# Z, B and C products of a token tower: the fifth pass split into two 64-row passes per bank, two sequences' passes side by side

## The chip, the cores and the metric

The kernel runs on one core of a Trainium2 chip. The metric is the device time of one execution in microseconds (us); the median of several runs is compared. Engines: PE is TensorE's matmul side and PEld its weight loads, DVE is VectorE, ACT is ScalarE, POOL is GpSimd, SP is SyncE. PSUM, where TensorE writes, has eight banks of 128 partitions x 512 float32.

## The reference, cut to what matters

8,192 tokens in 32 sequences of 256 are embedded (192 features) and pass through four layers, then one attention block (12 heads) and a small quantised feed-forward. The change touches the four layers only, where each layer computes

```
h  = layernorm(x) * g + b
uv = h @ Wi.T + bi ; u, v = halves of uv (192 features each)
uc = causal convolution of u over time, 4 taps, per feature
delta = softplus(uc @ Wd.T + bd)          # "Z" in the kernel
Bm = uc @ WB.T + bB ; Cm = uc @ WC.T + bC # "B" and "C"
y[t] = sum over features of state[t] * Cm[t],  state = state * exp(-delta) + uc * Bm
x  = x + (y * sigmoid(v)) @ Wout.T + bout
```

All products are wanted in nearly full float32.

## The kernel before, in words

**Iterations.** A chunk is two sequences (512 tokens). Each layer handles 16 chunks, so there are 64 layer iterations; `steps` writes them out for every engine, partly as an unrolled lead-in, partly as a loop. In one step every engine works on several chunks at different stages: on PE, `step` calls `uv(at(2))`, `z_c(at(3))`, `transposes(at(1))`, `rows(at(4))`, `b_c(at(3))` in this order. The order on each engine is fixed by the program, and semaphores (`wait(pe, name, count)`) are the only link between engines.

**Layout.** Features stand on partitions, time on the free axis. The 192 features are the 128 high ones (a whole tile) and 64 low ones. In `ucr_l` the low features of the two sequences share a tile: for the 256 columns of sequence b, the partitions `half(b)` (0 to 63 or 64 to 127) hold the rounded low features, and the other half holds what rounding left over. The weights `w_z[:, s, 1]` hold the 64 low input features twice, in both halves.

**Passes.** A product is a sum of passes accumulated in one bank, each a 128x128 weight load (LDWEIGHTS) and a matmul with 512 columns: rounded high features, `ucr_l` (both halves), the rest of the high features `ucr_r`, and then the rest of the weights `w_z_rest` times `ucr_h` and, fifth, times `ucr_l`. `z_product` (matmul line L706) does this five times for a column group. `z_c` calls it for the high Z rows (`Z_H`, bank `B_ZH`) and for the low Z and C rows together (`Z_LC`, bank `B_ZCL`). `b_c` calls it for `B_H` (bank `B_BH`) and `C_H` (bank `B_CH`); between them `b_low_product` (L717) makes the low B rows in bank `B_BL`, with 256 columns per pass and five passes for each of the two sequences. So an iteration has four products of five 512-column passes and ten 256-column passes on these lines.

**Other PE work in an iteration.** `uv_product` (L697) has three products of five 512-column passes; `transposes` (L758) has twelve 128-column ones; `rows` has matmuls on 128 rows (L787, L791) and then on 64 rows (L794, L797), taken alternately from the lower and the upper half of the partitions and written to different banks. `rows` stands directly ahead of `b_c`. In the attention block `scores` (L860) and `scores_t` (L873) also use 64-row operands, alternately in the lower and upper half, in two banks.

**Who reads what.** ACT's `decay` waits for `zh_done` (reads `B_ZH`, L1147) and then for `z_done` (reads `B_ZCL`, L1151 and L1155), then come `save_turned` (L1166), which waits for the transposes, and `round_rows` (L1176). DVE's `recurrence` (L1491 to L1518) waits for `b_done` and `c_done`; `rest_of_rows` is L1448, `save_y` L1526, `residual` L1537. `z_c` waits for `decay_ready` (the bank `B_ZCL` was read) between its two products; in one iteration each of the layers but the last it also waits there for `w_centred` and `w_biased`, since DVE's `centre_weights` (L1360, L1367) reads sums out of `B_ZCL`.

Of the kernel before, what the change touches and what calls it, by code (L numbers as in the profile page):

```python
# [17 lines left out]
HI, LO = 128, 64  # L18
S = 256
# [7 lines left out]
Z_H, Z_LC, B_PAD, B_H, C_H, Z_COLS = 0, 128, 256, 448, 576, 704  # L27

B_LOW = (B_PAD + 64, B_PAD)
# [11 lines left out]
def wait(eng, sem, value):  # L41

    if isinstance(value, int) and value <= 0:
        return
    eng.wait_ge(sem, value)


def build(nc, tokens, embedding, pos_enc, w_uv_d, w_z_d, w_o_d, gain_d, vec_d, bout, w_qkv_d, b_qkv_d, w_out_d,
# [9 lines left out]
    with ExitStack() as ctx:  # L58
# [6 lines left out]
        def sem(name):  # L65
            return ctx.enter_context(nc.semaphore(name))
# [34 lines left out]
        def sa(name, shape, dt=F32):  # L101
            return layers_memory.enter_context(nc.sbuf_tensor(name, shape, dt))
# [14 lines left out]
        w_z = sa("w_z", [P, 2, 2, Z_COLS], F32R)  # L117
        w_z_rest = sa("w_z_rest", [P, 2, 2, Z_COLS], F32R)
        ucr_h = sa("ucr_h", [P, 2, 2 * S], F32R)

        ucr_l = sa("ucr_l", [P, 2, 2 * S], F32R)
        ucr_r = sa("ucr_r", [P, 2, 2 * S], F32R)
# [111 lines left out]
        uc_ready = sem("uc_ready")  # L234
        sv_l_ready = sem("sv_l_ready")
        sv_ready = sem("sv_ready")
        zh_done = sem("zh_done")
        z_done = sem("z_done")
        dh_ready = sem("dh_ready")
        decay_ready = sem("decay_ready")  # L240
        b_done = sem("b_done")
        c_done = sem("c_done")
# [21 lines left out]
        def half(b):  # L264

            return slice(b * LO, (b + 1) * LO)
# [32 lines left out]
        def ahead(n, k):  # L299
            return min(n + k, ITEMS) if isinstance(n, int) else n + k  # L300
# [359 lines left out]
        def _(pe):  # L660
# [36 lines left out]
                    last = nc.tensor.matmul(out[:], w, r[:], start=(k == 0), stop=(k == len(passes) - 1))  # L697
                return last

            def z_product(l, col, b, out):  # L700

                c, s = slice(col, col + HI), l % 2
                passes = ((w_z[:, s, 0, c], ucr_h), (w_z[:, s, 1, c], ucr_l), (w_z[:, s, 0, c], ucr_r),
                          (w_z_rest[:, s, 0, c], ucr_h), (w_z_rest[:, s, 1, c], ucr_l))
                for k, (w, r) in enumerate(passes):
                    last = nc.tensor.matmul(out[:], w, r[:, b, :], start=(k == 0), stop=(k == len(passes) - 1))  # L706
                return last

            def b_low_product(l, s, out):


                for b in range(2):
                    c, w_s, q = slice(B_LOW[b], B_LOW[b] + HI), l % 2, slice(b * S, (b + 1) * S)
                    passes = ((w_z[:, w_s, 0, c], ucr_h), (w_z[:, w_s, 1, c], ucr_l), (w_z[:, w_s, 0, c], ucr_r),
                              (w_z_rest[:, w_s, 0, c], ucr_h), (w_z_rest[:, w_s, 1, c], ucr_l))
                    for k, (w, r) in enumerate(passes):
                        last = nc.tensor.matmul(out[:, 0:S], w, r[:, s, q], start=(b == 0 and k == 0),  # L717
                                                stop=(b == 1 and k == len(passes) - 1))
                return last

            def uv(it):
                if it is None:
# [12 lines left out]
            def z_c(it, centred):  # L735
                if it is None:
                    return
                n, l, c, s = it
                wait(pe, uc_ready, n + 1)
                wait(pe, x_updated, n - 1)  # L740
                z_product(l, Z_H, s, B_ZH).then_inc(zh_done, 1)
                wait(pe, decay_ready, n)
                if centred is not None:
                    pe.wait_ge(w_centred, 3 * (centred + 1))
                    pe.wait_ge(w_biased, 2 * centred + 1)
                z_product(l, Z_LC, s, B_ZCL).then_inc(z_done, 1)

            def transposes(it):
                if it is None:
# [51 lines left out]
            def b_c(it):  # L801
                if it is None:
                    return
                n, l, c, s = it
                wait(pe, ht_ready, ahead(n, 3))
                z_product(l, B_H, s, B_BH)
                b_low_product(l, s, B_BL).then_inc(b_done, 1)
                z_product(l, C_H, s, B_CH).then_inc(c_done, 1)

            def qkv_mean(part):  # L810

# [171 lines left out]
            def step(at, l, k):  # L983
                first = l == L and k == 2
                uv(at(2))
                if l == L - 1 and k in QKV_CENTRE:
                    pe.wait_ge(qkv_centred, 3 * (QKV_CENTRE.index(k) + 1))
                z_c(at(3), prepared(l, k, PREP_CENTRE))
                transposes(at(1))
                if first:  # L990

                    pe.wait_ge(qkv_split, 2)
                    pe.wait_ge(sv_ready, ITEMS)
                    turn_x1(seq(0), False)
                    turn_x1(seq(0), True)
                rows(at(4))
                if first:
                    project_qk(seq(0), 0)
                b_c(at(3))
                if first:  # L1000
                    project_qk(seq(0), 1)
                    pe.wait_ge(qk_saved, 1)
                    project_v(seq(0))
                    pe.wait_ge(qk_saved, 2)
                    turn_x1(seq(1), False)

                if l == L - 1 and k in QKV_MEANS:
                    wait(pe, decay_ready, at(3)[0] + 1)
                    qkv_mean(QKV_MEANS.index(k))
                if (to := prepared(l, k, PREP_MEANS)) is not None:  # L1010
                    wait(pe, decay_ready, at(3)[0] + 1)
                    means_of_sums(to)
# [819 lines left out]
```

## Time and profile before

| | |
|---|---|
| median of 3 runs | 1590.33 us (1590.24 to 1594.37) |
| the profiled execution's own time | 1598.23 us |
| its span, first to last instruction | 1596.3 us |
| mean granted TensorE clock | 0.977 |
| four layers, about | the first 965 us |
| attention and feed-forward | the rest |

The profile describes one execution. A matmul's recorded duration holds a modelled tail that overlaps the next matmul, so what a pass costs in a dense stretch is read from start to start. A weight load can run under the matmul before it. "Idle before" is the time for which an engine had nothing running, with what released it. Line numbers are those of the kernel before.

### The profile page before, as it was taken

The page shows a single profiled execution, that of the slowest core. Times are in us where ns is not written, and L with a number is a line of the kernel's source. Part 1 is how long each engine was busy: PE and PEld are TensorE (multiplying, and loading weights), DVE is VectorE, ACT ScalarE, POOL GpSimd, SP SyncE. Part 2 cuts the span into 40 slices and gives each one's busy share as a digit, 9 for nine tenths or more (in the row PEclk, how much of TensorE's full clock was granted, in tenths as well). Part 3 has the DMA queues.
Part 4 walks back from the last instruction along what each step waited for, and adds up shares of the span by engine and source line. Part 5 has one row for each costly group of instructions (what it writes and reads, how often), then busy time and mean ns, then how long its engine had stood idle before and what let it go on. Part 6 is the DMA issues. An engine that isn't in the chain of part 4 may idle for free.

```text
span 1596.3 us, 36428 instructions
## 1 busy us (share of the span) xinstructions
PE 1506.3 (94%) x11313; PEld 1232.6 (77%) x11313; DVE 1349.4 (85%) x3201; ACT 1241.8 (78%) x2686; POOL 836.2 (52%) x1428
## 2 busy tenths in 40 slices
PE   2699999999999999999999998999999999999986
PEld 1588878888888888888888886677777777777763
DVE  4699999999999999999999886678888878888763
ACT  2688878888888888888888963777787877877762
POOL 7777755443334453333333236566666666666642
PEclk9799999999999999999999997999999999999996
DMA  5311100000000000000000000000000000000000
GB/s 111 80 29 30 30 23 34 1 34 0 0 1 1 1 1 0 0 1 1 1 1 0 1 1 1 2 8 12 12 10 15 11 11 10 10 10 15 11 12 25
DMA packets 16571, 22.41 MB, mean 14 GB/s; under 512 B 2912, under 2 KB 13792, under 8 KB 16480
## 3 DMA queue, kind: packets, MB, share of 16 engines
q1 hardware_dynamic: 13408, 14.98, 2.8%
q0 software_dynamic: 3072, 6.30, 2.6%
q8 instruction: 48, 0.79, 0.2%
q14 instruction: 43, 0.35, 0.1%
HBM read 14.58 MB, written 6.29 MB: 13 GB/s over the span
## 4 chain that ended last, share of the span: by engine, by line
PE 60%; DVE 18%; ACT 9%; issue 9%; POOL 2%; DMA 1%; DVEq 1%; ACTq 0%; POOLq 0%
PE banks L706 9%; PE banks L921 7%; PE banks L697 7%; PE banks L889 6%; PE banks L846 5%; PE banks L873 5%; PE banks L860 4%; DVE hs_h L1500 3%; DVE x L1537 3%; DVE xs L1448 2%; PE banks L787 2%; PE banks L717 2%; PE banks L832 2%; PE banks L945 2%; PE banks L835 2%
## 5 line engine op out<-in xcount | busy, mean ns | idle before, releaser
L1593 DVE TENSOR_REDUCE mx<-banks 128x4 f32<-128x1024 f32 x192 | 234.2, 1220 | 45.6 <-PE banks L860 45.1
L1224 ACT ACTIVATE probs<-banks 128x1024 f32<-128x1024 f32 x192 | 195.7, 1019 | 84.5 <-PE banks L873 81.1
L503 POOL TENSOR_TENSOR x<-x,bo_row 128x768 f32<-128x768 f32 (+1 forms) x64 | 118.3, 1848 | 159.0 <-DVE ucr_r L1474 159.0
L697 PE MATMUL banks<-ht,w_uv 128*128 128x512 f32 x576 | 166.3, 398 | 14.3 <-ACT sv_l L1199 12.5
L479 POOL TENSOR_TENSOR lnt<-mv,const 128x4 f32<-128x4 f32 x64 | 20.4, 319 | 269.1 <-DVE mv L1439 268.8
L1465 DVE SCALAR_TENSOR_TENSOR uc_h<-u_h,vec,uc_h 128x512 f32<-128x512 f32 x192 | 146.9, 765 | 0.9 <-ACT uc_h L1137 0.9
L697 PEld LDWEIGHTS banks<-ht,w_uv 128*128 128x128 f32 x576 | 108.4, 191 | 42.0 <-issue 18.1
L1448 DVE SCALAR_TENSOR_TENSOR xs<-x,rstd,xs 128x192 fp32r<-128x192 f32 x256 | 89.9, 413 | 46.5 <-ACT xs L1176 46.5
L697 PE MATMUL banks<-ht,w_uv_rest 128*128 128x512 f32 x384 | 120.0, 394 | 0.0
L1116 ACT ACTIVATE u_l<-banks,vec 64x256 f32<-64x256 f32 x128 | 60.0, 469 | 73.5 <-PE banks L697 72.7
L873 PE MATMUL banks<-q_t,k_t 64*128 64x256 f32 x768 | 108.8, 334 | 7.7 <-ACT probs L1224 6.3
L706 PE MATMUL banks<-ucr_h,w_z 128*128 128x512 f32 x256 | 107.6, 420 | 4.5 <-issue 2.8
L846 PE MATMUL banks<-identr,parts 128*128 128x128 f32 x768 | 105.0, 261 | 4.2 <-issue 3.3
L1465 DVE SCALAR_TENSOR_TENSOR uc_l<-u_l,vec,uc_l 128x256 f32<-128x256 f32 x192 | 95.2, 496 | 12.1 <-POOL rstd L491 3.9
L1166 ACT ACTIVATE ht<-banks 128x512 fp32r<-128x512 f32 x192 | 100.8, 598 | 5.0 <-PE banks L758 3.5
L889 PE MATMUL banks<-probs,v_aug 128*32 128x256 f32 x1536 | 104.5, 390 | 0.0
L1133 ACT ACTIVATE uc_l<-banks,vec 64x256 f32<-64x256 f32 x128 | 71.7, 560 | 42.1 <-DVE inp_l L1494 41.0
L758 PEld LDWEIGHTS banks<-identr,xs 128*128 128x128 f32 x768 | 74.5, 142 | 38.0 <-DVE xs L1448 19.1
L1176 ACT ACTIVATE xs<-x,rstd 128x192 fp32r<-128x192 f32 (+1 forms) x256 | 95.6, 445 | 9.9 <-POOL rstd L491 8.3
L758 PE MATMUL banks<-identr,xs 128*128 128x128 f32 x768 | 77.6, 247 | 27.2 <-DVE xs L1448 19.0
L860 PE MATMUL banks<-k_t,q_t 64*128 64x256 f32 x768 | 94.7, 303 | 6.6 <-DVE mx L1593 2.6
L706 PE MATMUL banks<-ucr_l,w_z 128*128 128x512 f32 x256 | 101.0, 394 | 0.0
(191 smaller groups left out, 4662.8 us busy)
## 6 DMA issues: line engine op xcount, KB each, us to landing
out_dram<-y_out SPq DMA_DIRECT2D x32, 192.0 KB, 2.0
raw_z<-w_z_dram SPq DMA_DIRECT2D x4, 704.0 KB, 5.3
raw_uv<-w_uv_dram SPq DMA_DIRECT2D x4, 576.0 KB, 3.9
emb<-embedding_dram,idx POOLq DMA_INDIRECT x64
q_t<-mx_t SPq DMA_DIRECT2D x64, 6.0 KB
emb<-w_qkv_dram SPq DMA_DIRECT2D x1, 864.0 KB
w_o<-w_o_dram SPq DMA_DIRECT2D x1, 768.0 KB
bo_row<-bout_dram SPq DMA_DIRECT2D x4, 96.0 KB
```

What stands on the lines that cost most here:

```text
L503: nc.gpsimd.tensor_tensor(rows, rows, bo_row[:, l, :][:, None, :].broadcast_to([P, CT, D]), ALU.add).then_inc(x_biased, 1)
L697: last = nc.tensor.matmul(out[:], w, r[:], start=(k == 0), stop=(k == len(passes) - 1))
L706: last = nc.tensor.matmul(out[:], w, r[:, b, :], start=(k == 0), stop=(k == len(passes) - 1))
L758: last = nc.tensor.transpose(B_T[g][:, k * P:(k + 1) * P].bitcast(F32R), xs[:, k, g * P:(g + 1) * P], identr[:])
L846: last = nc.tensor.transpose(B_HEADS[g][:, (2 * o + t) * P:(2 * o + t + 1) * P].bitcast(F32R), parts[:, s, t, o, 2 * g:2 * g + 2, :].rearr ...
L860: last = nc.tensor.matmul(B_S[j][:, t * S:(t + 1) * S], q_t[q, s, g, t * P:(t + 1) * P], k_t[q, s, g, :], start=True, stop=True)
L873: last = nc.tensor.matmul(B_ST[j][:, t * S:(t + 1) * S], k_t[q, s, g, t * P:(t + 1) * P], q_t[q, s, g, :], start=True, stop=True)
L889: last = nc.tensor.matmul(bank[32 * h:32 * h + 32, c:c + S], v_aug[:, s, t, 4 * p + h, :], probs[:, (s + p) % 2, h // 2, (2 * (h % 2) + t) ...
L1224: act.activation(probs[:, (s + g // 2) % 2, g % 2, :].rearrange("p (j k) -> p j k", j=2), B_SST, ACT.Exp, scale=float(DH) ** -0.5).then_in ...
L1448: last = nc.vector.scalar_tensor_tensor(out=xs[:, k, D:2 * D], in0=x[:, tile_of(c, k)], scalar=rstd[:, s, k:k + 1], in1=xs[:, k, 0:D].bitc ...
L1465: nc.vector.scalar_tensor_tensor(out=uc, in0=uk, scalar=v(l, part, V_W0 + k), in1=uc, op0=ALU.mult, op1=ALU.add).then_inc(taps, 1)
L1593: nc.vector.tensor_reduce(mx[:, s].rearrange("p t (j h) -> p j t h", j=2)[:, :, :, g], B_SS.rearrange("p j (t k) -> p j t k", t=2), AX, AL ...
```

## The change

`z_product` and `b_low_product` go. Each product's first four passes stay as they are (`full_passes`). The fifth is replaced by one `low_pass` per sequence: weights and data only from the 64 partitions `half(b)` that hold the rounded low features, 256 columns. The product of the two leftovers is thus no longer computed. Two low passes are issued one after the other, one for each half of the partitions, into different banks. New semaphores `z_low` and `bc_low` keep PE from writing a bank from the other half before the first low pass has ended. The wait for `decay_ready`, `w_centred` and `w_biased` now stands ahead of all of `z_c`.

```diff
-            def z_product(l, col, b, out):
...
-            def b_low_product(l, s, out):
...
+            def full_passes(l, col, s, q, out, first, last):
+
+                c, w_s = slice(col, col + HI), l % 2
+                passes = ((w_z[:, w_s, 0, c], ucr_h), (w_z[:, w_s, 1, c], ucr_l), (w_z[:, w_s, 0, c], ucr_r),
+                          (w_z_rest[:, w_s, 0, c], ucr_h))
                 for k, (w, r) in enumerate(passes):
+                    done = nc.tensor.matmul(out, w, r[:, s, q], start=first and k == 0,
+                                            stop=last and k == len(passes) - 1, skip_group_check=True)
+                return done
+
+            def low_pass(l, col, s, b, out, first, last):
+                c, w_s = slice(col, col + HI), l % 2
+                return nc.tensor.matmul(out, w_z_rest[half(b), w_s, 1, c], ucr_l[half(b), s, b * S:(b + 1) * S],
+                                        start=first, stop=last, skip_group_check=True)
+
+            BOTH = slice(0, 2 * S)
+
+            def seq_of(bank, b):
+                return bank[:, b * S:(b + 1) * S]
...
                 wait(pe, x_updated, n - 1)
-                z_product(l, Z_H, s, B_ZH).then_inc(zh_done, 1)
                 wait(pe, decay_ready, n)
                 if centred is not None:
                     pe.wait_ge(w_centred, 3 * (centred + 1))
                     pe.wait_ge(w_biased, 2 * centred + 1)
-                z_product(l, Z_LC, s, B_ZCL).then_inc(z_done, 1)
+                low_pass(l, Z_H, s, 0, seq_of(B_ZH, 0), True, False).then_inc(z_low, 1)
+                low_pass(l, Z_LC, s, 1, seq_of(B_ZCL, 1), True, False).then_inc(z_low, 1)
+                full_passes(l, Z_H, s, BOTH, B_ZH[:], False, False)
+
+                wait(pe, z_low, 2 * (n + 1))
+                low_pass(l, Z_H, s, 1, seq_of(B_ZH, 1), False, True).then_inc(zh_done, 1)
+                low_pass(l, Z_LC, s, 0, seq_of(B_ZCL, 0), False, False)
+                full_passes(l, Z_LC, s, BOTH, B_ZCL[:], False, True).then_inc(z_done, 1)
...
                 wait(pe, ht_ready, ahead(n, 3))
-                z_product(l, B_H, s, B_BH)
-                b_low_product(l, s, B_BL).then_inc(b_done, 1)
-                z_product(l, C_H, s, B_CH).then_inc(c_done, 1)
+                low_pass(l, B_H, s, 0, seq_of(B_BH, 0), True, False).then_inc(bc_low, 1)
+                low_pass(l, C_H, s, 1, seq_of(B_CH, 1), True, False).then_inc(bc_low, 1)
+                full_passes(l, B_H, s, BOTH, B_BH[:], False, False)
+                wait(pe, bc_low, 3 * n + 2)
+                low_pass(l, B_LOW[0], s, 0, B_BL[:, 0:S], True, False).then_inc(bc_low, 1)
+                low_pass(l, B_H, s, 1, seq_of(B_BH, 1), False, True)
+                for b in range(2):
+                    full_passes(l, B_LOW[b], s, slice(b * S, (b + 1) * S), B_BL[:, 0:S], False, False)
+                wait(pe, bc_low, 3 * (n + 1))
+                low_pass(l, C_H, s, 0, seq_of(B_CH, 0), False, False)
+                low_pass(l, B_LOW[1], s, 1, B_BL[:, 0:S], False, True).then_inc(b_done, 1)
+                full_passes(l, C_H, s, BOTH, B_CH[:], False, True).then_inc(c_done, 1)
```

## Rows read from the trace of the kernel before

**Rows 1.** The page, section 1: busy time, share of the span, instructions of each engine.
```profile
PE 1506.3 (94%) x11313; PEld 1232.6 (77%) x11313; DVE 1349.4 (85%) x3201; ACT 1241.8 (78%) x2686; POOL 836.2 (52%) x1428
```

**Rows 2.** Windows, whole iterations: length, busy time (instructions), clock, DMA share, GB/s.
```profile
73.12:100.83 27.71, 27.59 (x180) 24.46 (x179) 25.63 (x62) 23.81 (x48) 20.23 (x28) 1.00 0.19 41
100.83:200.83 100.00, 97.25 (x624) 85.85 (x623) 99.08 (x239) 83.37 (x169) 76.30 (x97) 1.00 0.16 28
200.83:362.90 162.07, 156.78 (x997) 136.10 (x996) 155.43 (x393) 134.75 (x275) 80.45 (x109) 1.00 0.07 23
362.90:513.84 150.94, 150.94 (x981) 134.45 (x980) 140.45 (x375) 130.53 (x265) 51.88 (x88) 1.00 0.00 1
513.84:587.30 73.46, 71.39 (x454) 62.00 (x453) 70.26 (x180) 61.55 (x126) 36.93 (x50) 1.00 0.00 1
738.24:768.20 29.96, 29.96 (x187) 25.44 (x185) 27.80 (x74) 24.02 (x49) 9.68 (x17) 1.00 0.01 1
```
(The engines' order is PE, PEld, DVE, ACT, POOL.)

**Rows 3.** Waits of PE, 60 to 970 us: total us, times, longest.
```profile
PE banks L758 <- DVE hc_h L1514: 8.0, 17, 1.5
...
PE banks L697 <- ACT sv_l L1199: 1.8, 7, 0.4
```

**Rows 4.** Timeline of PE in one iteration: start, length, line, operation, shape.
```profile
604.47 0.39 PE L706 MATMUL banks<-ucr_h,w_z 128*128 128x512 f32 x1
604.70 0.39 PE L706 MATMUL banks<-ucr_l,w_z 128*128 128x512 f32 x1
...
606.51 0.39 PE L706 MATMUL banks<-ucr_l,w_z_rest 128*128 128x512 f32 x1
...
610.98 0.25 PE L797 MATMUL banks<-ones,hc_l 64*128 64x1 f32 x2
611.17 0.50 PE L706 MATMUL banks<-ucr_h,w_z 128*128 128x512 f32 x1
611.51 0.39 PE L706 MATMUL banks<-ucr_l,w_z 128*128 128x512 f32 x1
...
612.43 0.28 PE L717 MATMUL banks<-ucr_h,w_z 128*128 128x256 f32 x1
612.55 0.28 PE L717 MATMUL banks<-ucr_l,w_z 128*128 128x256 f32 x1
```

**Rows 5.** Timeline of PE in the attention block, in short windows around 1203 us.
```profile
1202.80 0.34 PE L921 MATMUL banks<-w_qkv_rest,h_t 128*128 128x384 f32 x1
...
1202.98 0.34 PE L921 MATMUL banks<-w_qkv_rest,h_t 128*128 128x384 f32 x1
1203.25 0.39 PE L873 MATMUL banks<-q_t,k_t 64*128 64x256 f32 x2
...
1203.47 0.28 PE L873 MATMUL banks<-q_t,k_t 64*128 64x256 f32 x2
1203.59 0.32 PE L860 MATMUL banks<-k_t,q_t 64*128 64x256 f32 x2
...
1203.75 0.28 PE L860 MATMUL banks<-k_t,q_t 64*128 64x256 f32 x2
1203.96 0.44 PE L945 MATMUL banks<-ident,o_t 128*128 128x128 f32 x2
```

**Rows 6.** Timeline of ACT, then of DVE, from the iteration of rows 4 on.
```profile
604.01 1.13 ACT L1133 ACTIVATE uc_l<-banks,vec 64x256 f32<-64x256 f32 x2 [0.57 <-DVE inp_l L1494]
...
606.98 0.94 ACT L1151 ACTIVATE dc_l<-banks,vec 64x256 f32<-64x256 f32 x2
...
612.04 1.41 DVE L1448 SCALAR_TENSOR_TENSOR xs<-x,rstd,xs 128x192 fp32r<-128x192 f32 x4 [0.64 <-ACT xs L1176]
...
617.06 0.47 DVE L1494 SCALAR_TENSOR_TENSOR inp_l<-banks,vec,uc_l 128x256 f32<-128x256 f32 x1
```

**Rows 7.** Timeline at the first layer boundary: DVE centring, PE's high Z product.
```profile
220.61 0.55 DVE L1367 TENSOR_TENSOR vec<-vec,banks 128x1 f32<-128x1 f32 x4
...
220.43 0.39 PE L706 MATMUL banks<-ucr_h,w_z 128*128 128x512 f32 x1
```

More of the change, by code:

```diff
@@ L236, in build @@
         sv_ready = sem("sv_ready")
+        z_low = sem("z_low")
+        bc_low = sem("bc_low")
         zh_done = sem("zh_done")
@@ L698, in uv_product @@
                 return last
-            def z_product(l, col, b, out):
-                c, s = slice(col, col + HI), l % 2
-                passes = ((w_z[:, s, 0, c], ucr_h), (w_z[:, s, 1, c], ucr_l), (w_z[:, s, 0, c], ucr_r),
-                          (w_z_rest[:, s, 0, c], ucr_h), (w_z_rest[:, s, 1, c], ucr_l))
+            def full_passes(l, col, s, q, out, first, last):
+                c, w_s = slice(col, col + HI), l % 2
+                passes = ((w_z[:, w_s, 0, c], ucr_h), (w_z[:, w_s, 1, c], ucr_l), (w_z[:, w_s, 0, c], ucr_r),
+                          (w_z_rest[:, w_s, 0, c], ucr_h))
                 for k, (w, r) in enumerate(passes):
-                    last = nc.tensor.matmul(out[:], w, r[:, b, :], start=(k == 0), stop=(k == len(passes) - 1))
-                return last
-            def b_low_product(l, s, out):
[L712 to L719, printed above, removed]
+                    done = nc.tensor.matmul(out, w, r[:, s, q], start=first and k == 0,
[8 more added lines that the diff above has]
+                return bank[:, b * S:(b + 1) * S]
             def uv(it):
```

## The prediction

> **What bounds the kernel now.** I read the windows first, cut at whole layer iterations (an iteration starts where PE starts a new u/v product). In the stretch from 362.90 to 513.84 PE is busy for all of 150.94 us; two more such stretches follow (587 to 738 and 768 to 919), so three times eleven iterations of 13.72 us have a PE that never idles, at a granted clock of 1.00 [rows 2]. The reader should not take "busy" for "at its peak", but here it is enough: no wait separates the matmuls, so anything PE does longer or shorter moves these 33 iterations one for one, as far as no other engine sets the pace. The list of PE's waits agrees: over all four layers it waits 8.0 us for DVE's `hc_h`, 17 times, and 1.8 us for ACT's `sv_l`, 7 times [rows 3]; these fall in the first layer and at the layer boundaries, where PE's busy time is below the window's (97.25 of 100.00, 156.78 of 162.07, 71.39 of 73.46) [rows 2].
>
> Then I asked what stands right behind PE. On ACT and DVE there is a ring: ACT starts `uc_l` when DVE's `inp_l` ended, at 604.01; from there it works without a gap to `xs`, which releases DVE at 612.04; DVE then works without a gap to the next `inp_l`, which ends at 617.06 + 0.47 = 617.53 [rows 6]. That is 13.52 us around, with no PE in it. PE's iteration is 13.72. So a faster PE could win at most about 0.2 us per iteration, while a slower PE costs its full price. This asymmetry decides much of the forecast.
>
> **What the change takes away.** A 512-column pass costs 604.70 - 604.47 = 0.23 us, a 256-column pass 612.55 - 612.43 = 0.12 us [rows 4]. Per iteration the fifth passes go: two of 512 in `z_c` (0.46), two of 512 and two of 256 in `b_c` (0.70). Together 1.16 us.
>
> **What it adds.** Ten 64-row, 256-column passes in five pairs. The trace has this very form in the attention block, alternating between halves and banks. The two members of a pair start together (one row, x2, at each time), and a pair follows the pair before after 1203.59 - 1203.47 = 0.12 us [rows 5]. So the pairs do run side by side: five pairs by 0.12 are 0.60 us. On columns alone the change would win 1.16 - 0.60 = 0.56 us per iteration.
>
> But the same rows show what it costs to go from 128-row to 64-row operands and back. (a) Into it: passes of 384 columns follow each other after 1202.98 - 1202.80 = 0.18 us, the 64-row pair comes 0.27 us after the last one: 0.09 more. (b) The first pair's weight load is not hidden: the second pair comes 1203.47 - 1203.25 = 0.22 us after the first instead of 0.12: 0.10 more. (c) Out of it: the next 128-row matmul comes 1203.96 - 1203.75 = 0.21 us after the last pair instead of 0.12: 0.09 more [rows 5]. (d) The first full pass's weight load is not hidden either: in `b_c` the second pass follows the first after 611.51 - 611.17 = 0.34 us instead of 0.23: 0.11 more [rows 4]. An excursion of one pair between full passes costs 0.09 + 0.10 + 0.12 + 0.09 + 0.11 = 0.51 us.
>
> `z_c` gets two excursions, since full u/v passes stand ahead of it and full transposes behind: 2 x 0.51 = 1.02, less 0.46 taken away: +0.56 us. `b_c` gets two excursions within it, 1.02 us, and its first pair joins the 64-row matmuls that `rows` ends with. Now the first full pass of `b_c` comes 611.17 - 610.98 = 0.19 us after the last L797 pair [rows 4]; with the low pair between, I take 0.12 to reach it and 0.21 to leave it: +0.14 us. Less 0.70: +0.46 us. Sum per iteration: +1.02 us of PE time, 14.74 us in place of 13.72. Bounds from both sides: if nothing but the columns counted, -0.56 (pairs at the cadence of [rows 5]); if members of a pair did not overlap at all, +1.02 + 5 x 0.12 = +1.62. I take +1.02, since each of its terms is measured on the same shape.
>
> What could make a step cheaper is that the waiting weight load is fetched early. The Trainium skill, TensorE: Matmul & The Clock Gate, section "Part 2: What happens when you issue a matmul", says that a weight load is pulled ahead of running matmuls when the row groups don't conflict or when it goes to the background buffer. By that rule (b) and (d) would vanish. The trace disagrees at every crossing I read: second members come 0.10 and 0.11 us late.
>
> **Edits that cost nothing.** PE's waits for `z_low` and `bc_low` stand behind four full passes (0.92 us) or eight short ones (0.96 us) that are issued after the pair they wait for; a pair ends within 0.3 us of its start (0.28 us is the longest record of a steady one [rows 5]), so PE still has queued work when the wait opens. Behind them in PE's queue stand the rest of `z_c` and everything after it; if a wait did bite, it would cost a part of a pair's length, under 0.3 us each. The wait for `decay_ready` moves ahead of the high Z product, by 1.15 us; ACT sets it two steps after `dc_l`, which starts at 606.98 [rows 6], so before 610, and it is wanted an iteration after 604.47, at 618.2. `w_centred` and `w_biased` move too, in three iterations: at the first boundary `w_biased` is set at 220.61 + 0.55 = 221.16 and `z_c` starts at 220.43 [rows 7], so PE would stand 0.7 us; it waits 8.0 us for `hc_h` in all, up to 1.5 at once [rows 3], and that longest wait comes right after, at 225, so this comes out of it. No DMA is moved; POOL and SP issue what they did.
>
> **What is late next.** ACT: `z_done` now comes with the last pass at 606.51 + 0.39 = 606.90 and `dc_l` starts at 606.98 [rows 4, 6]. After the change `z_done` is 0.56 later against the start of PE's iteration, so ACT stands some 0.5 us there, and the rest of the ring moves: `dc_l` to the end of DVE's residual some 9.6 us later (ACT 606.98 to 612.04, then DVE's `xs` to the residual, which ends ahead of `inp_h`, some 0.7 us before `inp_l` at 617.06 [rows 6]), then PE's high u product and `z_c`, 1.15 + 2.3 + 0.56, some 13.7 us around in all. That is below 14.74: ACT and DVE now wait for PE and PE for nobody.
>
> **The sum.** 33 iterations by 1.02 = 33.7 us. The first layer's seven at 100.00 / 7 = 14.29 us: there PE already idles, and 14.74 - 14.29 = 0.45 each, 3.2 us. The first two (27.71 us): 0.9 + 0.7 = 1.7 us. The eleven from 200.83 average 14.73 and are uneven: on PE's timeline five of them are 13.8 to 14.0 long and get 0.7 to 0.9 each, 4.1 us; six are 14.7 to 16.5 long, and their waits for DVE and ACT absorb the addition. The five from 513.84: 1.7 us by the same reading; the two from 738.24: 0.7 us. The one from 919 nothing, the three at the edges of the layers' span some 1.5 us. Sum 33.7 + 3.2 + 1.7 + 4.1 + 1.7 + 0.7 + 1.5 = 46.6 us. The attention block is untouched. On the profiled execution 1598.2 becomes 1645; it stood 7.9 us above the median of the runs, so I put the same 46.6 on the median: 1590.3 + 46.6 = 1637 us. Its own range is 1622 to 1650.
>
> **Rivals.**
> 1. *Only the drain is paid, the weight loads hide.* Then (b) and (d) go: four excursions by 0.21 less, so +0.18 us per iteration; 33 x 0.18 = 6, and little elsewhere: +8, 1598 us. Against it: [rows 4, 5] show both exposed.
> 2. *Faster: the switches cost nothing with 512-column passes between them.* PE then needs 13.72 - 0.56 = 13.16 us, and the ring of ACT and DVE becomes the bound at 13.52 [rows 6]. The gain is 0.2 us in 33 iterations, 6.6 us, plus a little of PE's waits: 1583 us. It decides if the switch price per iteration (1.58 now) is under 0.56. The page TensorEngine Tiling (Array Packing) of the Trainium skill, section "Theoretical Speedup", promises up to 2x for contractions of 64 rows, which is this case's arithmetic; nothing in the trace speaks for a free switch.
> 3. *Nothing is absorbed, or PE's added time brings further waits.* All 64 iterations pay 1.02, 65 us, or the ACT delay at `dc_l` reaches `ht` or `xs` and comes back to PE, or the granted clock sags: 1655 to 1665 us. For it: ACT's order is fixed, and at boundaries its weight rounding is in the ring. Against it: the ring has a microsecond of room after the change.
> 4. *The change doesn't do what it says:* pairs don't overlap. +1.62 per iteration, 33 x 1.62 + about 20 for the others: 1664 us. Against it: the x2 rows [rows 5].
>
> **Chances and range.** Forecast 0.74; rival 1 0.06; rival 2 0.03; rival 3 0.13; rival 4 0.04. The range 1614 to 1656 leaves out rivals 1, 2, 4 and half of 3. A measurement of this kernel tells 0.3%, some 5 us, from no change. Faster 0.03; within 0.3% 0.03; slower 0.94.
>
> **What would show it.** PE's instructions go from 11313 [rows 1] to about 11569 (four more per iteration). Steady iterations are 14.7 us long, still without a PE wait; each low pair starts about 0.3 us after the last full pass, and the next full pass 0.3 us after the pair, its successor 0.34 after it. ACT waits some 0.5 us at `dc_l` on PE. DVE idles about a microsecond more per iteration. The layers end near 1012 us rather than 965. The forecast is wrong if steady iterations come out under 14.4 or over 15.0 us, or if PE shows waits inside `z_c` and `b_c`.

## The result, and the profile after

The median went from 1590.28 to 1650.64 us; the ratio is 1.0363 (95% interval 1.0341 to 1.0386). The forecast was 1637 us with a range of 1614 to 1656 us: the direction and the mechanism held, and the size was 13.6 us short. The narrower range of the forecast itself, 1622 to 1650 us, was missed by 0.6 us; the stated range is wider because it takes in half of rival 3. A steady iteration of 14.87 us lies between the 14.4 and 15.0 us beyond which I had called the forecast wrong. The profiled execution of the kernel after took 1651.6 us with a span of 1649.7, against 1598.2 and 1596.3 before.

The page, section 1, and the windows of the kernel after, cut at the same iterations as [rows 2] (the columns are those of that group):

```profile
PE 1572.2 (95%) x11569; PEld 1210.8 (73%) x11569; DVE 1350.2 (82%) x3201; ACT 1252.4 (76%) x2686; POOL 827.8 (50%) x1428
```
```profile
71.68:101.42 29.74, 29.74 (x187) 23.80 (x186) 26.82 (x63) 24.09 (x48) 20.87 (x29) 1.00 0.19 47
101.42:205.55 104.13, 104.13 (x652) 83.32 (x651) 99.55 (x239) 84.32 (x168) 75.02 (x98) 1.00 0.16 27
205.55:372.67 167.12, 166.65 (x1041) 133.15 (x1039) 155.60 (x393) 137.09 (x274) 79.78 (x109) 1.00 0.07 22
372.67:536.26 163.59, 163.59 (x1024) 130.91 (x1023) 140.20 (x375) 132.49 (x264) 50.37 (x89) 1.00 0.00 0
536.26:611.97 75.71, 75.71 (x475) 60.56 (x473) 70.65 (x180) 62.46 (x125) 36.38 (x50) 1.00 0.00 1
611.97:775.60 163.63, 163.63 (x1025) 130.94 (x1024) 140.22 (x375) 132.47 (x264) 50.37 (x89) 1.00 0.00 1
775.60:807.98 32.38, 32.38 (x196) 24.87 (x194) 27.90 (x75) 24.10 (x48) 10.05 (x17) 1.00 0.00 1
807.98:971.72 163.74, 163.74 (x1024) 131.02 (x1024) 138.63 (x367) 134.08 (x267) 46.52 (x82) 1.00 0.00 1
```

PE runs 11569 matmuls, four more per iteration as predicted. It is now busy for the whole window nearly everywhere, in the first layer too, where it idled before [rows 2]. DVE's and ACT's busy times hardly moved. A steady iteration takes 163.59 / 11 = 14.87 us instead of 13.72.

The timeline of PE through one steady iteration; compare [rows 4] and [rows 5]:

```profile
644.69 0.61 PE L699 MATMUL banks<-ht,w_uv_rest 128*128 128x512 f32 x2
645.24 0.39 PE L717 MATMUL banks<-ucr_l,w_z_rest 64*128 64x256 f32 x2
645.55 0.49 PE L708 MATMUL banks<-ucr_h,w_z 128*128 128x512 f32 x1
645.89 0.39 PE L708 MATMUL banks<-ucr_l,w_z 128*128 128x512 f32 x1
646.12 0.40 PE L708 MATMUL banks<-ucr_r,w_z 128*128 128x512 f32 x1
646.35 0.40 PE L708 MATMUL banks<-ucr_h,w_z_rest 128*128 128x512 f32 x1
646.67 0.39 PE L717 MATMUL banks<-ucr_l,w_z_rest 64*128 64x256 f32 x2
646.99 0.50 PE L708 MATMUL banks<-ucr_h,w_z 128*128 128x512 f32 x1
...
648.03 1.12 PE L768 MATMUL banks<-identr,xs 128*128 128x128 f32 x12
...
652.36 0.37 PE L717 MATMUL banks<-ucr_l,w_z_rest 64*128 64x256 f32 x2
652.65 0.50 PE L708 MATMUL banks<-ucr_h,w_z 128*128 128x512 f32 x1
652.99 0.39 PE L708 MATMUL banks<-ucr_l,w_z 128*128 128x512 f32 x1
```

Both members of a low pair start together (x2 at one time). A pair in the middle starts 646.67 - 646.35 = 0.32 us after the last full pass (0.23 between full passes), the next full pass 646.99 - 646.67 = 0.32 us after the pair, and in the first excursion the pass behind that 645.89 - 645.55 = 0.34 us later. The profile shows no idle time of PE in any of these steps.

The weight loads at the two kinds of low pair, in the Z product and behind `rows`:

```profile
645.24 0.19 PEld L717 LDWEIGHTS banks<-ucr_l,w_z_rest 64*128 64x128 f32 x2 [0.35 <-issue]
645.55 0.19 PEld L708 LDWEIGHTS banks<-ucr_h,w_z 128*128 128x128 f32 x1
645.66 0.19 PEld L708 LDWEIGHTS banks<-ucr_l,w_z 128*128 128x128 f32 x1
...
652.33 0.19 PEld L717 LDWEIGHTS banks<-ucr_l,w_z_rest 64*128 64x128 f32 x2
652.65 0.19 PEld L708 LDWEIGHTS banks<-ucr_h,w_z 128*128 128x128 f32 x1
```

At a change of row mode (from 128-row to 64-row matmuls or back) the load starts with its own matmul (645.24, 645.55), so nothing of it lies under other work; within one mode the next load starts 0.23 us ahead of its matmul (645.66 against 645.89). The rule of the Trainium skill, TensorE: Matmul & The Clock Gate, section "Part 2: What happens when you issue a matmul", that a load is pulled ahead of running matmuls when row groups don't conflict or it goes to the background buffer, is seen within a mode and at none of the crossings read here.

Who waits for whom over the layers of the kernel after (us in all, times, longest):

```profile
ACT u_l L1137 <- PE banks L699: 100.4, 58, 3.3
DVE xs L1469 <- ACT xs L1197: 94.7, 55, 3.5
...
ACT dc_l L1172 <- PE banks L708: 24.8, 60, 0.4
ACT dc_h L1168 <- PE banks L717: 21.2, 49, 3.8
```

ACT waits at `dc_l` in 60 iterations, 0.41 us each, and at `dc_h` too; DVE waits for ACT. PE's own waits in the layers fell to 2.9 us for `ht`, 2.6 of them a single wait ahead of the first steady iterations, and 0.2 us for `hc_h`. What [rows 3] showed is gone: with more work per iteration PE comes later, and what it waited for is there.

### The profile page after: what moved, and what is told of

Same layout as the page of the kernel before. It is cut to its first block, busy times and chain, and to the rows that moved or that the text cites. A ratio compares the mean times of both kernels' runs of the same rounds, so it can differ in the third digit from the quotient of the medians.

```text
span 1649.7 us, 37033 instructions
## 1 busy us (share of the span) xinstructions
PE 1572.2 (95%) x11569; PEld 1210.8 (73%) x11569; DVE 1350.2 (82%) x3201; ACT 1252.4 (76%) x2686; POOL 827.8 (50%) x1428
## 4 chain that ended last, share of the span: by engine, by line
PE 90%; DVE 3%; POOL 2%; issue 2%; ACT 2%; DMA 0%; ACTq 0%; DVEq 0%; POOLq 0%
PE banks L708 21%; PE banks L699 13%; PE banks L942 7%; PE banks L910 6%; PE banks L717 6%; PE banks L797 5%; PE banks L867 5%; PE banks L894 5%; PE banks L881 4%; PE banks L768 3%; PE banks L804 3%; PE banks L801 3%; PE banks L853 2%; PE banks L856 2%; PE banks L966 2%
## 5 line engine op out<-in xcount | busy, mean ns | idle before, releaser
L708 PE MATMUL banks<-ucr_h,w_z 128*128 128x512 f32 (+1 forms) x384 | 171.0, 445 | 0.0
L708 PE MATMUL banks<-ucr_r,w_z 128*128 128x512 f32 (+1 forms) x384 | 137.9, 359 | 0.0
L708 PE MATMUL banks<-ucr_l,w_z 128*128 128x512 f32 (+1 forms) x384 | 137.2, 357 | 0.0
L708 PE MATMUL banks<-ucr_h,w_z_rest 128*128 128x512 f32 (+1 forms) x384 | 137.2, 357 | 0.0
L717 PE MATMUL banks<-ucr_l,w_z_rest 64*128 64x256 f32 x640 | 122.2, 378 | 2.9 <-ACT ht L1187 2.9
L717 PEld LDWEIGHTS banks<-ucr_l,w_z_rest 64*128 64x128 f32 x640 | 60.1, 184 | 81.7 <-issue 70.0
L708 PEld LDWEIGHTS banks<-ucr_h,w_z 128*128 128x128 f32 x384 | 71.9, 187 | 41.3 <-issue 0.2
```

Of the source, the lines that this page charges most:

```text
L708: done = nc.tensor.matmul(out, w, r[:, s, q], start=first and k == 0, stop=last and k == len(passes) - 1, skip_group_check=True)
L717: return nc.tensor.matmul(out, w_z_rest[half(b), w_s, 1, c], ucr_l[half(b), s, b * S:(b + 1) * S], start=first, stop=last, skip_group_chec ...
```

## Experiments

An excursion is the way from 128-row matmuls to 64-row ones and back; each has two crossings. "Z" below is the time from the last high u pass to the first transpose, "B/C" from the last L797 pair to the next u/v product, medians over eight to ten steady iterations, worked out from the starts in PE's timeline (for e5 the B/C time is left out, since PE waits in it):

| kernel | iteration | Z | B/C | ratio to before (95%) |
|---|---|---|---|---|
| before | 13.71 | 2.50 | 3.79 | 1 |
| after | 14.88 | 3.11 | 4.34 | 1.0363 (1.0341 to 1.0386) |
| e1, all passes 128 rows | 13.77 | 2.56 | 3.80 | 1.0016 (1.0002 to 1.003) |
| e2, 64 rows in Z alone | 14.33 | 3.11 | 3.80 | 1.0183 (1.0162 to 1.0203) |
| e3, 64 rows in B/C alone | 14.30 | 2.55 | 4.33 | 1.0162 (1.0142 to 1.0183) |
| e4, Z pairs taken apart | 15.87 | 4.12 | 4.33 | 1.0779 (1.0764 to 1.0795) |
| e5, no fifth pass | 13.63 | 2.05 | | 0.9988 (0.9975 to 1.0) |
| e6, both grouped | 14.72 | 3.06 | 4.23 | 1.0396 (1.0381 to 1.0411) |
| e7, B/C in four slots | 13.82 | 2.50 | 3.89 | 1.0044 (1.0031 to 1.0056) |
| e8, Z grouped | 14.27 | 3.06 | 3.79 | 1.0133 (1.0109 to 1.0158) |
| e9, B/C grouped | 14.15 | 2.50 | 4.23 | 1.0257 (1.0233 to 1.028) |

**e1: the order and the waits without the row modes.**

```diff
+            def wide_pass(l, col, s, b, out, first, last):
+                c, w_s = slice(col, col + HI), l % 2
+                return nc.tensor.matmul(out, w_z_rest[:, w_s, 1, c], ucr_l[:, s, b * S:(b + 1) * S],
+                                        start=first, stop=last, skip_group_check=True)
...
-                low_pass(l, Z_H, s, 0, seq_of(B_ZH, 0), True, False).then_inc(z_low, 1)
+                wide_pass(l, Z_H, s, 0, seq_of(B_ZH, 0), True, False).then_inc(z_low, 1)
...
```


> The kernel after in its new order, with its new waits and its ten low passes, but each low pass takes all 128 partitions (weights and data), so it is again the product of before and there is no change of row mode. Theory (the price is the change between 128-row and 64-row matmuls): ten 256-column passes cost what the fifth passes cost before, a steady iteration is 13.7 to 13.8 us and the time 1590 to 1594 us. Rival (the price is the order, the new waits, or the wait for decay_ready moved ahead): the iteration stays near 14.9 us and the time near 1650 us.

Eleven steady iterations of e1:

```profile
586.17:737.62 151.45, 151.45 (x1024) 136.36 (x1024) 140.49 (x375) 131.07 (x265) 51.68 (x88) 1.00 0.00 1
```

And its Z product, from the last high u pass to the first transposes, without a crossing:

```profile
603.13 0.39 PE L699 MATMUL banks<-ht,w_uv_rest 128*128 128x512 f32 x1
603.36 0.40 PE L723 MATMUL banks<-ucr_l,w_z_rest 128*128 128x256 f32 x2
...
605.70 0.29 PE L774 MATMUL banks<-identr,xs 128*128 128x128 f32 x2
```

151.45 us against 150.94 before and 163.6 after, with the 1024 matmuls of the kernel after. The order, the semaphores, the split of the fifth pass into two of 256 columns and the moved wait cost 0.06 us per iteration in all, and by the table they cost it in the Z product (2.56 against 2.50; B/C 3.80 against 3.79); the other 1.1 us is the 64-row form. The rival is refuted. The median, 1595.62 us, lies 2 us above my range; the kernel before had 1593.5 us on that chip, 3 us more than the median I had reckoned from.

**e2 and e3: one half each.** e2 keeps `low_pass` in `z_c` and takes `wide_pass` in `b_c`; e3 is the reverse.

> 64-row low passes in the Z products alone; those of B and C take all 128 partitions, the order is that of the kernel after. Theory (each excursion into 64-row mode costs 0.51 us with its pair): two excursions, 1.02 us, less 0.46 of full passes: PE iteration 14.3 us, 33 iterations by 0.6 and about 4 us elsewhere: 1612 to 1618 us. A rival that puts the price in B and C (a wait in their longer chain) expects under 1600 us.

> 64-row low passes in the B and C products alone, those of Z take all 128 partitions. Theory: two excursions and a first pair behind the 64-row matmuls of rows, 1.02 + 0.22 - 0.70 = +0.54 us: PE iteration 14.25 us, 1608 to 1616 us. With e2 the two gains in iteration length must add up to that of the kernel after (14.87 - 13.71 = 1.16), while the times add up to less than 60 us, since the first layer and the boundaries absorb a part twice.

Each half costs its part and leaves the other alone: over e1, e2 adds 14.33 - 13.77 = 0.56 us and e3 0.53, together 1.09 of the 14.88 - 13.77 = 1.11 us of the kernel after. The two ratios' gains add to 3.45%, under the 3.63% of the kernel after, as expected if waits absorb a part twice; with 0.2% to either side of each the intervals can't confirm it. The profiles show it: the first layer's seven iterations take 100.3 us in e2 and 100.3 in e3 against 100.0 before, so either half alone is absorbed there, but 104.1 in the kernel after. The medians, 1621.65 and 1618.2 us, lie 4 and 2 us above the tops of my ranges, again with the 1593.5 us of that chip to be set against 1590.3.

**e4: a dose of two more excursions.**

```diff
                 low_pass(l, Z_H, s, 0, seq_of(B_ZH, 0), True, False).then_inc(z_low, 1)
+                full_passes(l, Z_H, s, BOTH, B_ZH[:], False, False, (0, 1))
                 low_pass(l, Z_LC, s, 1, seq_of(B_ZCL, 1), True, False).then_inc(z_low, 1)
-                full_passes(l, Z_H, s, BOTH, B_ZH[:], False, False)
+                full_passes(l, Z_H, s, BOTH, B_ZH[:], False, False, (2, 3))
...
                 low_pass(l, Z_H, s, 1, seq_of(B_ZH, 1), False, True).then_inc(zh_done, 1)
+                full_passes(l, Z_LC, s, BOTH, B_ZCL[:], False, False, (0, 1))
                 low_pass(l, Z_LC, s, 0, seq_of(B_ZCL, 0), False, False)
...
```


> The kernel after with the two members of each Z pair taken apart: two full passes of the same product stand between them. Same instructions, same columns, two more excursions into 64-row mode per iteration. Theory: each single low pass in an excursion of its own costs 0.51 us like a pair, so +1.02 us: steady iteration 15.9 us, 64 iterations by 1.02 on top of 1650: 1712 to 1718 us. Rival (the price goes with the number of low passes or with the waits): no change from 1650 us.

```profile
652.41:827.01 174.60, 174.60 (x1024) 133.10 (x1023) 140.18 (x375) 132.44 (x264) 50.46 (x89) 1.00 0.00 1
```

174.60 / 11 = 15.87 us per iteration, and a median of 1715.51 us. With the same matmuls, Z went from 3.11 to 4.12: 1.01 us for two excursions where 1.02 was expected. The price goes with the number of crossings.

**e5: the most that the change could win.** `z_product` and `b_low_product` of the kernel before without their fifth pass.

```diff
-                          (w_z_rest[:, s, 0, c], ucr_h), (w_z_rest[:, s, 1, c], ucr_l))
+                          (w_z_rest[:, s, 0, c], ucr_h))
...
```


> The kernel before without any fifth pass: the product of the weights' rest with the low features is left out. PE has 1.16 us less per iteration than before and no change of mode is added, so this is more than the change could ever win. My claim of a ring of ACT and DVE at 13.52 us: iteration 13.4 to 13.6 us, 1578 to 1586 us. Rival (PE alone sets the pace): iteration 12.6 us, 1525 to 1535 us.

```profile
587.10:737.16 150.06, 141.17 (x913) 122.59 (x914) 140.24 (x376) 130.05 (x265) 51.53 (x88) 1.00 0.00 1
```

And its waits of PE between 587 and 737 us:

```profile
PE banks L697 <- ACT sv_l L1199: 8.9, 11, 0.9
```

The chain of work that ended last, by line, in eleven steady iterations of the kernel before and then of e5 (the view cuts the second line off):

```profile
by line: PE banks L706 35.1%; PE banks L697 24.8%; PE banks L787 10.0%; PE banks L717 8.7%; PE banks L758 7.2%; PE banks L794 6.2%; PE banks L791 5.7%; PE banks L797 2.5%
by line: issue 23.5%; DVE x L1537 9.8%; ACT xs L1176 9.4%; ACT ht L1166 8.3%; DVE xs L1448 8.2%; ACT dc_l L1151 6.6%; DVE hs_h L1500 6.5%; DVE inp_h L1491 4.8%; ACT uc_h L1137 4.5%; ACT u_h L1122 4.5%; DVE inp_l L1494 2.3%; DVE ucr_l L1479 
```

PE's work fell by 1.16 us per iteration and the iteration by 0.08: PE is idle for 0.8 us per iteration until ACT has read the bank (`sv_l`). The chain is PE alone before, and holds no work of PE in e5 ("issue" is time in which an engine waited for nothing that the profile shows). So a ring of ACT and DVE bounds the kernel right behind PE, at 13.64 us rather than my 13.52. The rival, PE alone, is refuted. The time fell by 0.12% (0 to 0.25%), 2 us where I had expected some 8, and the median of 1590.21 us lies above my range. Part of what is missing is the clock. Near 535 us of the profiled execution the granted clock was at the lower of its two levels (1.2 in place of 2.4 GHz) for 10 us, right behind a wait of PE:

```profile
533.60 0.54 PE L758 MATMUL banks<-identr,xs 128*128 128x128 f32 x4 [1.46 <-DVE hc_h L1514]
534.65:544.89 10.24, 10.24 (x46) 9.63 (x45) 8.86 (x27) 7.76 (x17) 4.58 (x8) 0.50 0.00 1
```

This iteration and the next took 19.4 + 12.9 us against 15.5 + 13.8 at the same place in the kernel before, 3 us more. Whether the other executions of e5 had such a fall isn't on record. From these two numbers I estimate that the change could have won 2 to 5 us and no more.

**e6: all low passes grouped, with waits between pairs.** `z_c`: pair, wait, pair, eight full passes. `b_c`: pair, wait, pair, wait, pair, sixteen full passes.

```diff
...
                 low_pass(l, B_H, s, 0, seq_of(B_BH, 0), True, False).then_inc(bc_low, 1)
                 low_pass(l, C_H, s, 1, seq_of(B_CH, 1), True, False).then_inc(bc_low, 1)
-                full_passes(l, B_H, s, BOTH, B_BH[:], False, False)
                 wait(pe, bc_low, 3 * n + 2)
                 low_pass(l, B_LOW[0], s, 0, B_BL[:, 0:S], True, False).then_inc(bc_low, 1)
                 low_pass(l, B_H, s, 1, seq_of(B_BH, 1), False, False)
-                for b in range(2):
-                    full_passes(l, B_LOW[b], s, slice(b * S, (b + 1) * S), B_BL[:, 0:S], False, False)
                 wait(pe, bc_low, 3 * (n + 1))
...
```


> All low passes of z_c in one excursion ahead of both full products, and all of b_c right behind the 64-row matmuls of rows; a wait for the earlier pair stands between pairs that write one bank from both halves. Three excursions fewer than after (0.39 us each without their pair, 1.17 in all), three waits on a matmul's end more. A wait costs the pair's length of about 0.36 us instead of 0.12 and an unhidden weight load of 0.1, so about 0.35 each, 1.05 in all. Theory: about even with the kernel after, 1640 to 1650 us. Rival (excursions are not what costs): +1.05 us per iteration on top, 1700 us or more. If waits cost nothing: 1603 us.

The weight loads of the two grouped Z pairs:

```profile
647.67 0.19 PEld L717 LDWEIGHTS banks<-ucr_l,w_z_rest 64*128 64x128 f32 x2 [0.35 <-issue]
648.14 0.19 PEld L717 LDWEIGHTS banks<-ucr_l,w_z_rest 64*128 64x128 f32 x2 [0.29 <-PE banks L717]
```

Undisturbed iterations take 14.70 us, 0.17 less than those of the kernel after, so three excursions fewer were nearly all paid for by three waits, as expected. But the time is 1655.69 us, above the range given: nine iterations of the layers, about one in seven, take some 1.5 us longer (16.2), and in each of them the granted clock fell. Without these 13 us the time would lie in the range. That was not expected; e8 and e9 follow it.

**e7: four slots behind `rows`, Z as before.** As e6 in `b_c`, but the second slot holds `B_LOW[0]` alone and the last `B_LOW[1]` alone.

```diff
-                z_product(l, B_H, s, B_BH)
-                b_low_product(l, s, B_BL).then_inc(b_done, 1)
-                z_product(l, C_H, s, B_CH).then_inc(c_done, 1)
...
+                low_pass(l, B_H, s, 0, seq_of(B_BH, 0), True, False).then_inc(bc_low, 1)
+                low_pass(l, C_H, s, 1, seq_of(B_CH, 1), True, False).then_inc(bc_low, 1)
+                low_pass(l, B_LOW[0], s, 0, B_BL[:, 0:S], True, False).then_inc(bc_low, 1)
+                wait(pe, bc_low, 3 * n + 2)
+                low_pass(l, C_H, s, 0, seq_of(B_CH, 0), False, False)
+                low_pass(l, B_H, s, 1, seq_of(B_BH, 1), False, False)
+                wait(pe, bc_low, 3 * (n + 1))
+                low_pass(l, B_LOW[1], s, 1, B_BL[:, 0:S], False, False)
...
```


> z_c as in the kernel before. The six low passes of b_c stand behind the 64-row matmuls of rows in four slots (two pairs, two singles), arranged so that a bank is written from the other half only two slots later, with two waits. No excursion is added. Theory: 0.11 to reach the first, about 0.75 for the slots with their waits, 0.21 to leave, against 0.19 and 0.70 before: +0.2 us per iteration, 1596 to 1600 us. If the waits are hidden by the slot between: 0.11 + 0.48 + 0.21 - 0.89 = -0.1 us, 1586 to 1590 us.

```profile
611.54 0.96 PE L725 MATMUL banks<-ucr_l,w_z_rest 64*128 64x256 f32 x6
612.43 0.50 PE L716 MATMUL banks<-ucr_h,w_z 128*128 128x512 f32 x1
```

An iteration takes 13.82 us, 0.11 more than before and between my two figures; the median of 1598.74 us lies in the first range. Even with no added excursion the 64-row form loses here: from the first slot to the full passes PE needs 612.43 - 611.54 = 0.89 us, where three steps of 0.12 from slot to slot and 0.21 to leave would be 0.57 (the 0.48 of my second figure counts one step too many). The slots follow each other after 0.20, 0.25 and 0.23 us. How much of that is the waits and how much are weight loads that nothing hides was not taken apart.

**e8 and e9: which grouped stretch moves the clock.** e8 has the `z_c` of e6 and the `b_c` of before; e9 the reverse.

> z_c has its two low pairs in one excursion, with a wait between them, as in e6; b_c is that of the kernel before. In the trace of e6 the stretch from the last high u pass to the first transpose is 3.05 us against 2.50 before, so the iteration should be 14.26 us and the time 1608 to 1616 us. If one excursion with a wait were cheaper than two (the gain the grouping was meant for), it would be under 14.2. The granted clock of e6 fell for 3.4 us about every seventh iteration, each time seen after the 64-row stretch of b_c. If that stretch is what it answers to, no such fall is seen here between 100 and 960 us.

> z_c is that of the kernel before; b_c has its three low pairs directly behind the 64-row matmuls of rows, with two waits, as in e6. Iteration 13.71 + (14.70 - 14.26) = 14.15 us, 1604 to 1612 us, plus 1.5 us for each fall of the granted clock. If the 64-row stretch of b_c is what the clock answers to, the falls of e6 are seen here too (some nine between 100 and 1000 us, 13 us in all, so up to 1620 us); if it answers to the sum of both stretches, neither e8 nor e9 shows them.

The iterations came out at 14.27 and 14.15 us (undisturbed ones), as read off e6. e8 has no fall of the granted clock between 100 and 960 us. e9 has seventeen, nearly twice as many as e6, and takes 1635.91 us, above the range given; less 17 times 1.5 us it would lie in it. The median of e8, 1614.95 us, is in its range. In the traces of e6 and e9 all 26 falls start 0.6 to 1.7 us after the first low pair of a `b_c`. Windows of e9 around one fall:

```profile
643.40:646.80 3.40, 3.26 (x32) 2.71 (x31) 2.03 (x5) 3.36 (x9) 2.39 (x6) 0.99 0.00 0
646.80:650.20 3.40, 3.40 (x13) 3.01 (x13) 3.34 (x11) 2.40 (x5) 0.48 (x1) 0.51 0.00 0
650.20:653.60 3.40, 3.40 (x16) 2.79 (x16) 3.40 (x8) 1.15 (x3) 1.38 (x1) 1.00 0.00 0
```

and what PE did:

```profile
644.21 0.92 PE L812 MATMUL banks<-w_o,sv_l 64*128 64x192 f32 x8
644.96 0.51 PE L815 MATMUL banks<-ones,hc_l 64*128 64x1 f32 x8
645.33 1.28 PE L725 MATMUL banks<-ucr_l,w_z_rest 64*128 64x256 f32 x6
646.54 0.64 PE L716 MATMUL banks<-ucr_h,w_z 128*128 128x512 f32 x1
646.98 0.63 PE L716 MATMUL banks<-ucr_l,w_z 128*128 128x512 f32 x1
647.40 0.63 PE L716 MATMUL banks<-ucr_r,w_z 128*128 128x512 f32 x1
```

At the lower level the 512-column passes follow each other after 0.42 us instead of 0.23. So in these two kernels it is the stretch of `b_c` that the clock answers to, and the sum of both stretches is refuted as its cause. Why e6, with the same stretch, has only nine falls is open.

## Why the prediction was right, and what it missed

**The price of a crossing: right.** It came out within 0.01 us: 0.32 into the pair ((a): 0.23 + 0.09), 0.32 from pair to full pass ((b), (c) and the pair, measured only as a sum: 0.10 + 0.12 + 0.09 = 0.31), 0.34 behind it ((d)). e4 measured an excursion at 0.505 us against 0.51. e1 shows that without the row modes nothing else in the change costs more than 0.06 us.

**The first low pair of `b_c`: mis-sized.** I took 0.12 us to reach it and 0.21 to leave it. It is reached after 0.11, but left after 652.65 - 652.36 = 0.29. Behind the one-column matmuls its weight load starts only 0.03 us before the pair, so that hardly any of it is hidden; that this is what costs the 0.08 is my reading. e7 shows the same: its second slot comes 0.20 us after the first, not 0.12. That is 0.08 us per iteration; the row that gave 0.12 was a pair behind another 256-column pair.

**What I had put at nothing: the new order.** Z grew by 0.61 us where I had 0.56. The missing 0.05 is not in the crossings: e1, which has none, already needs 2.56 in Z against 2.50, and e2 adds 0.55 to that, where two excursions less the fifth passes were priced at 0.56. So "edits that cost nothing" cost 0.06 us; which of them (the order, the split into 256 columns, a wait) was not taken apart. In B/C e3 adds 0.53 to e1, against 0.46 + 0.08. The sum is 1.02 + 0.06 + 0.08 = 1.16, and 14.87 - 13.72 is 1.15.

**The sum over stretches.** By stretch, before to after, against my term: the three steady ones 38.1 us (33.7); the first layer's seven 4.1 (3.2); the first two 2.0 (1.7); the eleven from 200.83 5.1 (4.1); the five from 513.84 2.2 (1.7); the two from 738.24 32.4 - 30.0 = 2.4 (0.7); the rest 1.3 (1.5). Together 55.2 us in the layers, where 46.6 stood. Of the 8.6 us missing, the 0.13 us per iteration is 4.3 in the steady stretches and some 2 elsewhere, and the two iterations from 738.24 are 1.7. Those two were a misreading: [rows 2] had PE busy for 29.96 of 29.96 us there, so nothing could absorb the addition, and full price was due.

**From the profile to the median: missed by 7 us.** This is half of the 13.6 us, and no step of the kernel explains it. The profiled executions differ by 53.4 us (layers +55.2, the start 1.1 less, the attention block 0.9 less), the medians by 60.4. The profiled execution of before lay 7.9 us over its median, that of after 1.0 us. I carried the difference over as it stood. Part of it may be scatter: medians of the kernel before in later comparisons were 1593.5, 1591.3 and 1593.5 us.

**What hides what.** The waits for `z_low` and `bc_low` and the moved wait show no idle time of PE, as predicted, and together with the order they cost no more than 0.06 us (e1). One reading behind that was off: I took 0.28 us as the longest record of a pair, while [rows 5] have one of 0.32 and the low pairs here have 0.37 to 0.39; with more than 0.9 us of passes in between it made no difference. ACT's stall at `dc_l` was 0.41 us (0.5 predicted) and did not come back to PE; the stall at `dc_h` I had not named. The cap on a gain was right in kind; its place is 13.64 us instead of 13.52. The layers ended at 1019 us, not 1012, for the reasons above.

**Rivals.** 1 (only the drain): refuted by the load rows. 2 (faster): switches are not free, and e5 shows some 2 to 5 us to win at best. 3 (nothing absorbed): not as told. PE has no further waits, and 64 iterations at 1.15 would be 73.6 us where the layers grew by 55.2, so some 18 us were absorbed; but the time, 1650.64 us, is nearer to this rival's 1655 than to the forecast's 1637. 4 (pairs don't overlap): refuted by the x2 rows.

## What to carry to other kernels

Half-height passes do run two at a time here, 0.12 us for a pair of 256 columns instead of for one pass; but each trip from 128-row to 64-row matmuls and back costs 0.39 us besides, so by these figures (an estimate that no run here tested) a trip pays only with four or more pairs in it that need no wait between them. Before halving an engine's work, look for the second bound: with PE relieved of 1.16 us per iteration (e5), the iteration fell by 0.08. When a price is taken from another place in a trace, check that the neighbour ahead has the same shape: behind one-column matmuls the first pair cost 0.08 us more than behind a 256-column pair. And an edit that only reorders and splits passes should be given a price too; here it was 0.06 us.

## What was unexpected of the hardware

The granted clock fell to the lower of its two levels (0.51 from 646.80 to 650.20 in e9, 1.2 in place of 2.4 GHz) although PE was recorded busy nearly throughout. In all 26 cases in the layers, nine in e6 and seventeen in e9, PE had just run the 64-row matmuls of `rows`, one-column ones among them, and then, within 1.2 us, three low pairs with two waits between them (in one case the last pair was still to come). In e7, whose low stretch is 0.9 us with shorter waits, and in e8 no such fall occurs in the layers. The one fall in the layers of e5, which has no low pass, came behind an idle PE. Each fall lengthened an iteration of e9 by some 1.5 us (15.7 against 14.15). Whether the 64-row form or the waits count is open.

A wait of PE for its own earlier pair costs 0.32 to 0.35 us: in e6 the second Z pair starts 648.14 - 647.67 = 0.47 us after the first instead of 0.12, and in the `b_c` of e9 the second and third follow after 0.45 and 0.44 us.
